# Cross- and self-attention block in fp32 halves: softmax sums sent through DRAM, V's two halves in one stationary tile

## What is computed

```python
def attention(x, ctx, Wq, Wk, Wv, Wo, bo):
    q = (x @ Wq).reshape(b, n, HEADS, D_HEAD)
    k = (ctx @ Wk).reshape(b, m, HEADS, D_HEAD)
    v = (ctx @ Wv).reshape(b, m, HEADS, D_HEAD)
    sim = jnp.einsum('bihd,bjhd->bhij', q, k) * SCALE
    attn = jax.nn.softmax(sim, axis=-1)
    out = jnp.einsum('bhij,bjhd->bihd', attn, v).reshape(b, n, HEADS * D_HEAD)
    return out @ Wo + bo
h = layernorm(x, ln1_g, ln1_b);  x = attention(h, h, a1_Wq, a1_Wk, a1_Wv, a1_Wo, a1_bo) + x
h = layernorm(x, ln2_g, ln2_b);  x = attention(h, context, a2_Wq, a2_Wk, a2_Wv, a2_Wo, a2_bo) + x
h = layernorm(x, ln3_g, ln3_b)
u, gate = jnp.split(h @ ff_Wp + ff_bp, 2, axis=-1)
x = u * gelu(gate) @ ff_Wo + ff_bo + x
```

## Time and profile before

| | |
|---|---|
| median of 3 runs | 1039.62 us (1035.93 to 1044.18) |
| profiled execution | 1043.19 us, span 1041.4 us |
| mean granted clock of TensorE | 0.981 |
| busy share PE, DVE, ACT, POOL | 94%, 68%, 60%, 35% |
| first layer | span 0 to 182 us |
| self steps | 182 to 592 us |
| cross steps | 592 to 896 us |
| feed-forward | 896 to 1041 us |

### The profile page before, as it was taken

The page is one execution under the profiler, slowest core; times in us unless marked ns, Lnnn a source line. Parts: engine busy times, 40 slices in busy tenths (PEclk is TensorE's granted clock), DMA queues, the critical chain, the costliest instruction groups (busy, mean ns, idle before and its releaser), DMA issues.

```text
span 1041.4 us, 21195 instructions
## 1 busy us (share of the span) xinstructions
PE 976.7 (94%) x7776; PEld 916.2 (88%) x7776; DVE 706.4 (68%) x1594; ACT 624.6 (60%) x1945; POOL 365.6 (35%) x514
## 2 busy tenths in 40 slices
PE   4588979899999999999999999999999997999998
PEld 4577868799999999999999989999999997999998
DVE  3466767867676766666768776677677667666574
ACT  2566645866666666666667666776666667434343
POOL 1011444633333333333323344554455454401010
PEclk9999989999999999999999989999999999999999
DMA  7220201002100000000002100300000001000110
GB/s 214 71 71 1 76 1 51 32 2 64 39 22 1 22 1 21 2 21 2 22 1 75 33 27 1 107 26 9 19 26 26 2 22 61 21 21 25 39 32 21
DMA packets 30444, 34.60 MB, mean 33 GB/s; under 512 B 4360, under 2 KB 23816, under 8 KB 30344
## 3 DMA queue, kind: packets, MB, share of 16 engines
q1 hardware_dynamic: 30344, 33.26, 10.5%
HBM read 24.86 MB, written 8.39 MB: 32 GB/s over the span
## 4 chain that ended last, share of the span: by engine, by line
PE 79%; DVE 9%; ACT 8%; issue 2%; POOL 1%; SPq 1%; DMA 0%; DVEq 0%
PE bank L1386 14%; PE bank L1388 14%; PE bank L1387 14%; PE bank L1630 8%; PE bank L1609 5%; PE bank L1398 5%; PE bank L1672 3%; PE bank L1674 3%; PE bank L1673 3%; PE bank L1646 3%; ACT p L769 2%; PE bank L1502 1%; PE bank L1503 1%; PE bank L1504 1%; DVE hT_lo L1142 1%
## 5 line engine op out<-in xcount | busy, mean ns | idle before, releaser
L577 POOL TENSOR_TENSOR oT_hi<-oT,ones 128x256 fp32r<-128x256 f32 x128 | 93.9, 733 | 364.0 <-DVE oT L1182 364.0
L769 ACT ACTIVATE p<-bank,negmax 128x256 f32<-128x256 f32 (+1 forms) x512 | 207.8, 427 | 20.7 <-DVE negmax L1159 16.0
L779 ACT CAST pT_hi<-bank 128x512 fp32r<-128x512 f32 (+1 forms) x256 | 110.9, 486 | 165.6 <-PE bank L1630 165.3
L1386 PE MATMUL bank<-hT_hi,w_hi 128*128 128x256 f32 x640 | 188.5, 295 | 6.8 <-DVE hT_lo L1142 2.6
L1388 PE MATMUL bank<-hT_hi,w_lo 128*128 128x256 f32 x640 | 179.4, 280 | 0.0
L1387 PE MATMUL bank<-hT_lo,w_hi 128*128 128x256 f32 x640 | 179.1, 280 | 0.0
L1386 PEld LDWEIGHTS bank<-hT_hi,w_hi 128*128 128x128 f32 x640 | 121.6, 190 | 10.1 <-DVE hT_lo L1142 4.7
L1174 DVE TENSOR_TENSOR pT_lo<-bank,pT_hi 128x512 fp32r<-128x512 f32 (+1 forms) x256 | 129.5, 547 | 0.4
L1155 DVE TENSOR_REDUCE negmax<-bank 128x2 f32<-128x512 f32 x128 | 82.2, 683 | 66.9 <-PE bank L1609 66.9
L1387 PEld LDWEIGHTS bank<-hT_lo,w_hi 128*128 128x128 f32 x640 | 121.3, 190 | 0.0
L1388 PEld LDWEIGHTS bank<-hT_hi,w_lo 128*128 128x128 f32 x640 | 121.1, 189 | 0.0
(11 more groups left out here) (202 smaller groups left out, 2730.1 us busy)
## 6 DMA issues: line engine op xcount, KB each, us to landing
w_stage<-in_weights SPq DMA_DIRECT2D x47, 256.0 KB, 4.3
x_in<-x_dram SPq DMA_DIRECT2D x24, 256.0 KB, 2.9
x_dram<-x_out SPq DMA_DIRECT2D x16, 256.0 KB, 3.2
l_x<-in_x SPq DMA_DIRECT2D x4, 512.0 KB, 5.0
x_dram<-l_out SPq DMA_DIRECT2D x4, 512.0 KB, 2.8
out_dram<-x_out SPq DMA_DIRECT2D x8, 256.0 KB, 3.2
w_stage<-in_weights SPq DMA_DIRECT2D x9, 128.0 KB, 5.2
l_ctx<-in_ctx SPq DMA_DIRECT2D x4, 180.0 KB, 4.6
```

The costliest lines, as they stand in the source:

```text
L577: nc.gpsimd.tensor_tensor(oh[:, G % PAIRS, :], of[:, :], ones[:, :], ALU.mult).then_inc(y["o_hi"], 1)
L769: last = nc.scalar.activation(p[:, G % 2, e, t * cols:(t + 1) * cols], scores_at(G, e, t), ACT.Exp, bias=negmax[:, G % 2, t, e:e + 1], acc ...
L779: nc.scalar.copy(pTh[0:r, G % 2, e, 0:n], bank[4 + e][0:r, 0:n]).then_inc(y["pT_hi"], 1)
L1386: nc.tensor.matmul(dst, lh, rh, start=(i == 0), stop=False)
```

## The change

Parts, in the order of a step:

- V is stored once, `v_hi_lo`, with high and low part of a head side by side: for each pair the four 64-column pieces are high of head 0, low of head 0, low of head 1, high of head 1. One stationary tile of 128 columns is one head's both parts. A head's output then has its high-part product in one half of the partitions and its low-part product in the other; head 0 goes to the first half of bank 6, head 1 to the second. It takes two matmuls per head and key tile (p's high and p's low part), 8 in a self step and 4 in a cross step, and the term low x low is now in it. No zero columns, no memsets.
- ACT copies the low-part products (`copy_low_values`), 64 partitions of each head, to the partitions where the high ones stand. DVE adds them (`add_low_values`), two operations of 64x256, into one of four slots of `oT`. PE's next `weighted_values` waits for that add.
- The reciprocals go to DRAM and back: SP sends `rs` of step G (256 pieces of two values) to one of four rows in DRAM, and after the next step's send it reads them back with a broadcast to 64 partitions for each head, into one of four slots of `rsumT`. `widen_sums`, the two transposes and `copy_rT` are gone.
- POOL multiplies the sum by the reciprocals (`o_norm`), then rounds and subtracts as before.
- SP's program now walks over the steps. Loads and stores stand between the sends at fixed steps.

```diff
-VW = 3 * DH
+VW = 2 * DH
+DEEP = 4
...
+            def send_sums(G):
+                sp.wait_ge(y["rsum"], G + 1)
+                if G >= DEEP:
+                    sp.wait_ge(*spread_until(G - DEEP))
+                sp.dma_start(sums_dram[G % DEEP, :, :].rearrange("e (q t) -> q e t", t=NT),
+                             rs[:, G % 2, :].rearrange("q (e t) -> q e t", e=2)).then_inc(y[f"rsum_row{G % 2}"], 16)
+
+            def spread_sums(G):
+                sp.wait_ge(y[f"rsum_row{G % 2}"], 16 * (G // 2 + 1))
+                if G >= 2:
+                    sp.wait_ge(*spread_until(G - 2))
+                if G >= DEEP:
+                    sp.wait_ge(y["o_norm"], G - DEEP + 1)
+                for e in range(2):
+                    sp.dma_start(rT[e * DH:(e + 1) * DH, G % DEEP, :],
+                                 sums_dram[G % DEEP, e:e + 1, :].partition_broadcast(DH)).then_inc(y[f"rT{G % 2}"], 16)
...
+            for G in range(STEPS):
+                b, i = divmod(G, PAIRS)
+                send_sums(G)
+                if G >= 1:
+                    spread_sums(G - 1)
+                if G == 1:
+                    store_first(LAST)
+                if G == 3:
+                    sp.wait_ge(z["stored"], 16 * (NI + 1))
+                if i == 3 and b >= 1:
+                    store(b - 1)
+                if i == 4:
+                    load(b + 2)
+                if i == 5 and B < b + 2 < 2 * B:
+                    load_context(b + 2)
+                if b == 1 and i < 4:
+                    load_weights(sp, 12 + i, 13 + i)
...
             def split_o(G):
+                pool.wait_ge(y["o_sum"], G + 1)
+                pool.wait_ge(*spread_until(G))
+                if G >= 1:
+                    pool.wait_ge(y["o_lo"], G)
+                nc.gpsimd.tensor_tensor(on[:, :].rearrange("p (t q) -> p t q", t=NT),
+                                        of[:, G % DEEP, :].rearrange("p (t q) -> p t q", t=NT),
+                                        rT[:, G % DEEP, :].rearrange("p (q t) -> p t q", t=NT),
+                                        ALU.mult).then_inc(y["o_norm"], 1)
...
-            def copy_rT(G):
+            def copy_low_values(G):
                 act.wait_ge(y["o"], G + 1)
-                nc.scalar.copy(rT[:, :], bank[6][:, S:2 * S]).then_inc(y["rT_copied"], 1)
+                if G >= 1:
+                    act.wait_ge(y["o_sum"], G)
+                nc.scalar.copy(ob[0:DH, :], bank[6][DH:128, 0:S])
+                nc.scalar.copy(ob[DH:128, :], bank[6][0:DH, S:2 * S]).then_inc(y["o_low"], 1)
...
             def inverse_sums(G):
                 dve.wait_ge(y["exp"], 2 * G + 2)
+                if G >= 2:
+                    dve.wait_ge(y[f"rsum_row{G % 2}"], 16 * (G // 2))
...
-            def normalise_o(G):
-                dve.wait_ge(y["rT_copied"], G + 1)
-                if G >= 1:
-                    dve.wait_ge(y["o_lo"], G)
-                nc.vector.tensor_tensor(of[:, :], bank[6][:, 0:S], rT[:, :], ALU.mult).then_inc(y["o_norm"], 1)
+            def add_low_values(G):
+                dve.wait_ge(y["o_low"], G + 1)
+                if G >= DEEP:
+                    dve.wait_ge(y["o_norm"], G - DEEP + 1)
+                nc.vector.tensor_tensor(of[0:DH, G % DEEP, :], bank[6][0:DH, 0:S], ob[0:DH, :], ALU.add)
+                nc.vector.tensor_tensor(of[DH:128, G % DEEP, :], bank[6][DH:128, S:2 * S], ob[DH:128, :], ALU.add
+                                        ).then_inc(y["o_sum"], 1)
...
             def weighted_values(G):
-                pe.wait_ge(y["rsum_wide"], G + 1)
                 if G >= 1:
-                    pe.wait_ge(y["o_norm"], G)
-                for t in range(NT):
-                    nc.tensor.transpose(bank[6][:, S + t * 128:S + (t + 1) * 128], rsw[:, G % 2, t, :], ident[:, :])
...
-                product(bank[6][:, 0:S], terms).then_inc(y["o"], 1)
+                    pe.wait_ge(y["o_sum"], G)
+                for e in range(2):
+                    dst = bank[6][:, e * S:(e + 1) * S]
+                    for j in range(tiles):
+                        vs = vv[0:r, j, (2 * g + e) * VW:(2 * g + e + 1) * VW]
+                        pc = slice(j * S, (j + 1) * S)
+                        nc.tensor.matmul(dst, vs, pTh[0:r, G % 2, e, pc], start=(j == 0), stop=False)
+                        last = nc.tensor.matmul(dst, vs, pTl[0:r, G % 2, e, pc], start=False, stop=(j == tiles - 1))
+                last.then_inc(y["o"], 1)
```

More of the change, by code:

```diff
@@ L224, in build @@
             qkl = sb("qkT_lo", [128, PAIRS, 2, S], F32R, where=l1)
-            vh = sb("v_hi", [128, NT, PAIRS * VW], F32R, where=l1)
-            vl = sb("v_lo", [128, NT, PAIRS * VW], F32R, where=l1)
+            vv = sb("v_hi_lo", [128, NT, HEADS * VW], F32R, where=l1)
             p = sb("p", [128, 2, 2, NT * S], where=l1)
@@ L229, in build @@
             pTl = sb("pT_lo", [128, 2, 2, NT * S], F32R, where=l1)
[L230 to L232 removed]
+            rT = sb("rsumT", [128, DEEP, S], where=l1)
+            of = sb("oT", [128, DEEP, S], where=l1)
+            ob = sb("oT_low_values", [128, S], where=l1)
+            on = sb("oT_scaled", [128, S], where=l1)
             oh = sb("oT_hi", [128, PAIRS, S], F32R, where=l1)
             ol = sb("oT_lo", [128, PAIRS, S], F32R, where=l1)
+            sb("below_x_in", [128, 512], where=l1)
             xo = sb("x_out", [128, NT, D], where=l1)
@@ L279, in build, with spread_until @@
         LAST = NI - 1
+        sums_dram = nc.dram_tensor("rsums_dram", (DEEP, 2, S), F32, kind="Internal").ap()
+        def spread_until(G):
+            return y[f"rT{G % 2}"], 32 * (G // 2 + 1)
         def out_banks(it):
@@ L337, in v_src, with v_dst @@
             return v_bank(b, c)[0:v_rows(b), :].rearrange("p (g e d) -> p g e d", g=4, e=2)
-        def v_dst(buf, b, c):
-            half = slice(c % 2 * 4 * VW, (c % 2 + 1) * 4 * VW)
-            return buf[0:v_rows(b), c // 2, half].rearrange("p (g s d) -> p g s d", g=4, s=3)[:, :, 0:3:2, :]
+        def v_dst(b, c, low):
+            part = vv[0:v_rows(b), c // 2, c % 2 * 4 * 2 * VW:(c % 2 + 1) * 4 * 2 * VW]
+            part = part.rearrange("p (g s d) -> p g s d", g=4, s=4)
+            return part[:, :, 1:3, :] if low else part[:, :, 0:4:3, :]
         def first_c():
@@ L470, in _ @@
             store_first(2)
[L471 to L476, removed]
-                store(b)
[L478 to L487, removed]
+            for G in range(STEPS):
[15 more added lines that the diff above has]
+                    load_weights(sp, 12 + i, 13 + i)
+                if b == B - 1 and 2 <= i < 6:
+                    load_weights(sp, 14 + i, 15 + i)
+                if b == B + 1 and i < 4:
+                    load_weights(sp, 20 + i, 21 + i)
+                if b == 2 * B - 1 and i >= 6:
+                    load_weights(sp, 18 + i, 19 + i)
+            spread_sums(STEPS - 1)
+            store(2 * B - 1)
+            for b in range(2 * B, 3 * B):
+                if b + 2 < 3 * B:
+                    load(b + 2)
+                store(b)
             sp.wait_ge(y["stored"], 16 * (3 * B + 1))
@@ L544, in first_layer @@
                     add_bias(0)
[L545 to L549, removed]
                 if it >= 1:
@@ L800, in round_values @@
                 act.wait_ge(y["v"], value_product(b, c))
-                nc.scalar.copy(v_dst(vh, b, c), v_src(b, c)).then_inc(y["v_hi"], 1)
+                nc.scalar.copy(v_dst(b, c, False), v_src(b, c)).then_inc(y["v_hi"], 1)
             def step_self(G):
```

43 lines of the change are left out of this document (14 added, 29 removed).

## The result

The changed kernel takes 1045.35 us (median of 20 runs, 1041.51 to 1048.81); the kernel before, beside it, 1039.39. The ratio is 1.0056, interval 1.0041 to 1.0071: half a per cent slower, inside the 1% that counts as no change here. The forecast was 1010 us in a range of 985 to 1031. The profiled execution's span is 1042.5 us (before 1041.4).

A forecast was written before the change was run, and what follows sets the result against it. TensorE was taken to bound self batches without a gap, cross batches also waiting once on DVE. Self part -39.3 and cross and end +9.2 sum to -30.1 us: 1039.6 to 1009.5, say 1010, range 985 to 1031.

The forecast's parts named there:

- the price of the six plain cross batches: Six plain cross batches: -0.8 us each from the chain, +1.6 from clock falls, so +0.8 each, +5 in all.
- first and last self batch: Self part: DVE and ACT have almost no slack there; 1.5 and 3 us of PE's saving given back.
- PE's saving: Fewer matmuls and transposes on PE: 0.67 us saved per self step, 0.42 per cross step, 69.8 us in all.
- Durations: 64x256 copies and adds at full price (up to 0.39 and 0.42 us more per step), POOL's product 0.74, landings 2.9.
- Rival D: Sums' round trip through DRAM lands late, PE waiting in step 1's output projection: slower, 1068 us at a 9 us landing; chance 0.06.
- The idle in a cross batch: Plain cross batch: PE's gap in step 4 grows from 1.2 to 2.7 us, keys start 0.9 later; -0.8 instead of -3.4.
- The clock: Plain cross batches: granted clock falls after the gap in about two of three, mostly the short kind; on average 1.6 us each.
- rival C: Long falls of the clock in every cross batch: 1021 to 1032 us; chance 0.22.

The follow-up runs named there:

- experiment 4: Changed kernel plus 16 unread matmuls in step 4 of cross batches; one copy and one add left out from the fifth step on, self steps too: 1003.98 us.
- experiment 3: Kernel before, cross steps' ACT copy and DVE product each in two 64x256 pieces: 1079.83 us; with 16 unread matmuls in step 4 added, 1054.22 us.
- experiment 2: Changed kernel, cross steps with only one of two ACT copies and one of two DVE adds, every second head's output stale: 1028.64 us.
- experiment 7: Changed kernel, copies and adds moved ahead of splits in cross step 3 (last batch: weights' too): 1025.51 us; with 16 unread matmuls in step 4, 1019.51 us.
- experiment 1: Changed kernel, 16 matmuls that nothing reads put on PE in step 4 of every cross batch: 1030.67 us, ratio 0.9928.
- experiment 6: Changed kernel, copies right behind exponentials and adds behind p's low part in all cross steps: 1055.43 us; with 16 unread matmuls in step 4, 1053.77 us.

## Why the prediction was wrong

The step that failed is the price of the six plain cross batches: +5 us forecast, +26.2 measured. In it the granted clock's falls were put at 1.6 us per batch and came to 4.0, and the growth of PE's idle was put 0.8 too low. The second mis-sized term is the first and last self batch, 8.5 us. The wait and the fall behind it were the right mechanism.

- **PE's saving: right.** The six plain self batches were to give 6 x 8 x 0.67 = 32 us and gave 30.1 with PE busy 278.5 of 279.2. The cross batches' PE work shrank by about 18 us for 20.
- **Durations: right.** 64-partition operations cost what 128 partitions cost (copies 0.37, adds 0.41 and 0.43). The product took 0.74, the landings 2.8 and 3.2. Rival D did not come.
- **First and last self batch: mis-sized.** The prediction gave back 1.5 and 3 us and kept 4.8 and 2.4; 1.3 was lost and 0.0 kept, 8.5 us off. DVE went from 37.3 to 42.5 of 47.4 and from 43.2 to 47.8 of 54.1: the reading is that where DVE and ACT also split weights they set the pace, and each add shows. For the last self batch, half the chain gave back 1.6 of 2.4 (experiment 4). It also has a fall of the clock that it did not have before (0.97, one stretch of 3.4 us, 1.7 us at most), and so has the run of experiment 4. What the first batch went to is open, and about 1 us of it differs from run to run.
- **The idle in a cross batch: mis-sized.** The gap of 2.7 us in step 4 was close: in the batch above 2.24, and 0.65 in front of the keys. But the waits in steps 1 to 3 were booked at 0.8 and came to 1.9. Two things in the rows go that way, neither tested by itself: POOL's and DVE's results met PE everywhere it had got earlier, and the overlap of 0.05 between neighbours that made "about 0.7" of a step's chain was not there (0.37 + 0.37 + 0.40 + 0.43 back to back, +0.8). PE's idle grew by 20.6 / 6 = 3.4 us per batch; the -0.8 had room for 2.6.
- **The clock: the step that decided.** "One in about two of three batches, mostly the short kind", 1.6 us each: it fell in all six, never for the short 3.3 us, at 24 / 6 = 4.0 each by the length of the falls; the least that experiment 3 shows for a fall behind a gap like it is 3.7. This was rival C (0.22), mechanism and all. The oscillation that the Trainium skill describes (TensorE: Matmul & The Clock Gate, HAM oscillation), a loop that idles once per turn and starts every turn at half rate, is what the trace shows in each of the six batches, though here PE waits for DVE's add (1.76 to 2.63 us) and in the page's loop for a DMA. The sum had it at the short length. I had taken the length of a fall from the two falls of the kernel before, and put most weight on the shorter. The reason given against C, that behind the long fall PE was also waiting, is a misreading of the row: PE was busy for 10.03 of those 10.10 us, as it is for 6.80 of 6.80 in the stretch above.
- **C's own price was too low** (1021 to 1032), since the idle, the first and the last self batch came on top: 8.5 + 2.1 for the self part and 6 x 0.8 for the idle make 15 more, 1036 to 1047.

Together: 2.1 (plain self) + 8.5 + 21.2 (plain cross, +26.2 for +5), less 0.6 for the ends, is the 31.2 us between -30.1 and +1.1.

## To carry to other kernels

Taking work off the busiest engine pays in the stages where it never waits, and can cost more than it brings where it already waits once per turn for a chain through other engines, however idle these are on average: DVE was busy for 26.0 of 36.7 us in a cross batch and still set the wait. Such a regular wait may pull the clock down every turn. Price the fall at the long form that the trace has, and look at the order of the second engine first: its finished result may stand behind splits that nobody needs yet, and moving two of them (with the weights' in the last batch) was worth 20 us here. Move only what nobody waits for, and do the same to the old kernel before crediting the change: it gained some 9 us by it.

## What the runs showed of the hardware

- **Idle and clock.** One wait of 1.17 us per batch kept 1.00. With 2.12 per batch (experiment 3), 2.24 + 0.65 (after) and 1.36 + 0.65 (experiment 2; other batches more) the clock fell to 0.50 in every batch; with 0.73 + 0.64 (experiment 7) in four of six, for 3.4 us in three of them. One wait alone does not decide it: the gap of about 2 us at the start of the self steps left it at 1.00. 16 matmuls that nothing reads, about 1.9 us of work, were worth 15, 26 and 6 us (experiments 1, 3 and 7), and nothing that can be measured in experiment 6.
- **DVE beside POOL.** `hT_lo`, a subtraction of two SBUF tiles, took 1.27 us in the batch above while POOL ran `x_plus_bias`, and 0.69 where experiment 6 had moved it away from it. It is no cost of the change by itself: in the kernel before it took 1.11 to 1.13 in the same place, also beside `x_plus_bias`. In the cross batches of the changed kernel the one that starts second is the one that is slow: `hT_lo` took 1.27 to 1.65 where POOL had started first and 0.69 to 0.80 where it had started first itself, and then POOL's addition took up to 1.73 for its usual 1.27.

```profile
706.41 1.27 POOL L596 TENSOR_TENSOR x_plus_bias<-x_in,rows_bc 128x512 f32<-128x512 f32 x1
```

```profile
717.41 0.69 DVE L1178 TENSOR_TENSOR hT_lo<-xhat,hT_hi 128x512 fp32r<-128x512 f32 x1
```

The Trainium skill (SBUF — State Buffer, Who interferes with whom) says that a DVE instruction with two SBUF inputs contends with a GpSimd instruction that reads SBUF; these rows agree. How much of the 20 us of the new order is this half microsecond per batch was not separated.
